# The attention mask is written into the score banks by ScalarE instead of by TensorE, and the scores are laid out by head

## The chip, the cores and the metric

One NeuronCore of a Trainium2 chip, five engines: TensorE (PE, with its weight loads as PEld), VectorE (DVE), ScalarE (ACT), GpSimd (POOL) and SyncE (SP, which issues the DMAs). The metric is the device time of one execution in microseconds, lower is better.

## What is computed

A macaron block on 2048 tokens of 128 channels, all in float32: half a stack of six layers, a retention block, the same half stack again.

```
x = x + 0.5 * stack(layernorm(x))
x = x + retention(layernorm(x))
x = x + 0.5 * stack(layernorm(x))

def stack(x):                                   # 6 layers
    for i in range(6):
        x = attention(shift_tokens(x), ...) + x
        x = ffn(shift_tokens(x), ...) + x       # layernorm, 128 -> 2*341, a * gelu(gate), 341 -> 128

def attention(x):                               # 16 heads of 64, windows of 32
    q, k, v = split(x @ Wqkv); q = l2norm(q) * qs; k = l2norm(k) * ksc
    q, k = rotary with scales
    # each window of 32 queries sees its own 32 keys and the 32 before them
    sim = 8 * q @ k.T, masked where i < j, i > j + 32 or before the first window
    out = softmax(sim) @ v;  return out @ Wo
```

Wv and Wo are folded into one matrix per head when the kernel starts, so V is projected straight into 128 outputs per head.

## The kernel before

**Tiles and slots.** Tokens are cut into 16 tiles of 128 (four windows each). A stack runs 6 x 16 = 96 tiles, one new tile per slot, in a software pipeline: in slot c the projections of tile c, the first transposes of tile c-1, the mask and scores of tile c-2, the softmax of tile c-3, the V projection of tile c-4 and the attention of tile c-5 are done. The feed-forward part works on groups of four tiles, spread over four slots: `ffn_centre` and `ffn_variance` at c % 4 = 0, `ffn_up(.., 0)` at 1, `ffn_up(.., 1)` at 2, `ffn_up(.., 2)` and the three `ffn_down` at 3. At c % 16 = 7 `ffn_bias` is added. The program is unrolled; every engine has its own list and runs it strictly in the order written; only semaphores tie the lists together. `after(...)` and `need(...)` are waits for a count. The order of the list around the change is what matters here.

**TensorE in a slot** (from L986 on): `project_qk(0)`, `ffn_up(2)`, `attend` (tile c-5), `p_transpose(4, 1)`, `project_v(0)`, `project_v(1)`, `out_transpose`, `project_qk(1)`, `qk_transpose(1, 0)` and `(1, 1)`, `project_v(2)`, `(3)`, `project_qk(2)`, `ffn_down(0)`, `project_qk(3)`, `ffn_down(1)`, `ffn_centre`, `ffn_down(2)`, `ffn_bias`, `qk_transpose(2, 3)`, `mask_scores`, `qk_transpose(1, 2)`, `ffn_up(0 or 1)`, `scores`, `p_transpose(3, 0)`, `ffn_variance`.

**ScalarE in a slot** (L479 to L540): Gelu of the third up part; the attention's output copy; `p_out(4, 1)`; `v_out(0)` (L462), `square(0)` (L442), `v_out(1)`, `square(1)`; the exponential of tile c-3 (L503); `qk_out(1, 0)`, `qk_out(1, 1)` (L456); `v_out(2)`, `square(2)`, `v_out(3)`, `square(3)`, `qk_out(2, 3)`: the last copy of transposed keys into KT; the feed-forward's square, or its Gelu (L476) between two table loads; `qk_out(1, 2)` into QT; `p_out(3, 0)`; the logarithm and exponential of the norms.

**VectorE in a slot** (L640 to L708): rotary products `rotate(0)`, `rotate(1)` (L597, L602), two square sums (L610); sums of the softmax (L651), reciprocal; `rotate(2)`, `square_sum(2)`, `square_sum(3)`, a maximum with a constant over the norms (L661); `rotate(3)`; maximum of the scores (L671) and subtraction into Z (L675), which is signalled by `s_z`; `inverse_norm`; the feed-forward's residual; `attn_residual` (L629), which waits for `out_transpose` of the next slot's TensorE list.

**GpSimd in a slot** (L358 to L378): the rotary table, `norm_mult(1, 1)` (L337), `rot_add(0)` (L330), `norm_mult(1, 2)`, `rot_add(1)`, `softmax_mult`, `last_keys` (L354, at c % 4 = 1), `rot_add(2)`, `norm_mult(1, 3)`, `rot_add(3)`, `norm_mult(0, 0)`.

**Banks.** VS is two PSUM banks of 512 columns. They hold, one after the other in a slot, the V projection's outputs (L886) and the masked scores. Head 8e + ch has its 64 scores in bank e: 32 at ch*32 for the window before and 32 at 256 + ch*32 for its own. `mask_scores` (L914) opens both banks with a product of a bf16 identity and a bf16 mask of 0 and -1e30; the 64 products of `scores` (128 records in the profile, as each float32 product takes two) are added to it. TensorE must wait for `s_te3`, the count of `qk_out(.., 3)`, before `scores`, and for `s_z` of the tile before `project_v(0)`.

## Time and profile before

| | |
|---|---|
| median of 3 runs | 3583.01 us (3582.12 to 3585.25) |
| profiled execution | 3582.17 us, span of the core 3580.4 us |
| TensorE busy | 3406.9 us, 95% of the span |
| TensorE weight loads | 1859.3 us, 52% |
| VectorE busy | 2839.3 us, 79% |
| ScalarE busy | 2383.7 us, 67% |
| GpSimd busy | 2334.5 us, 65% |
| mean granted TensorE clock | 0.974 |
| chain that ended last | 91% TensorE; of its lines the mask's L920 has 2% |

The first slots start at 101.6 us (first stack) and 1893.3 us (second); before, between and behind lie the folding of weights, the layer norms and the retention block. Busy time is a union of the profiled spans; the ends of matmuls are modelled, so spans of successive products overlap, and the price of a product is the distance between starts.

### The profile page before, as it was taken

Reading aid. Unit: us, or ns where it says so; the run is one execution under the profiler, and the core shown is the slowest. Engines: PE = TensorE matmul, PEld = TensorE weight load, DVE = VectorE, ACT = ScalarE, POOL = GpSimd, SP = SyncE. Lnnn points to the kernel's source line nnn. Section 1 sums busy time; section 2 is a strip of 40 time slices with the busy share of each in tenths; the row PEclk is TensorE's granted clock in tenths of the full one; section 3 lists DMA queues with packets and bytes.
Section 4 is the critical chain, followed back from the end, with each engine's and each line's share of the span. In section 5 each row is a group of like instructions: output and inputs, shape, how many; then the busy total and the mean of one; then the engine's idle time right before and its main releaser. Section 6 shows DMA issues by size and latency. Waiting matters only on the chain.

```text
span 3580.4 us, 123150 instructions
## 1 busy us (share of the span) xinstructions
PE 3406.9 (95%) x51660; PEld 1859.3 (52%) x51660; DVE 2839.3 (79%) x6042; ACT 2383.7 (67%) x4153; POOL 2334.5 (65%) x2187
## 2 busy tenths in 40 slices
PE   3799999999999999999797999999999999999997
PEld 2355555555555555555363555555555555555553
DVE  1788888888888888888367888888888888888883
ACT  1566776776776776776524667767777767767764
POOL 0677766767766766767046767777777767777761
PEclk7799999999999999999898999999999999999998
DMA  5000000000000000000100000000000000000000
GB/s 192 9 11 27 23 12 27 23 12 27 22 13 27 22 13 27 21 13 4 56 1 9 10 28 21 12 28 21 12 29 21 12 28 21 12 28 22 12 5 13
DMA packets 50087, 82.93 MB, mean 23 GB/s; under 512 B 7168, under 2 KB 37120, under 8 KB 47232
## 3 DMA queue, kind: packets, MB, share of 16 engines
q1 hardware_dynamic: 49536, 75.05, 6.6%
q8 instruction: 411, 6.73, 0.8%
q14 instruction: 140, 1.15, 0.1%
HBM read 67.69 MB, written 7.34 MB: 21 GB/s over the span
## 4 chain that ended last, share of the span: by engine, by line
PE 91%; DVE 3%; issue 2%; ACT 1%; DMA 1%; POOL 1%; SPq 0%; DVEq 0%; POOLq 0%; ACTq 0%
PE VS L886 20%; PE QA L826 18%; PE TB L845 10%; PE TB L910 9%; PE VS L936 7%; PE TB L869 6%; PE FB L962 4%; PE FB L963 3%; PE FB L971 3%; PE VS L920 2%; PE TB L853 1%; PE FB L952 1%; PE FB L947 1%; DMA KT<-in_w_out 1%; DVE T L602 1%
## 5 line engine op out<-in xcount | busy, mean ns | idle before, releaser
L330 POOL TENSOR_TENSOR QN<-T 128x512 f32<-128x512 f32 x768 | 980.5, 1277 | 574.4 <-DVE T L602 574.4
L337 POOL TENSOR_TENSOR QN<-QN,RR 128x512 f32<-128x512 f32 x768 | 800.9, 1043 | 295.1 <-DVE RR L623 295.1
L826 PE MATMUL QA<-WQ,Y 128*128 128x512 f32 x1536 | 796.6, 617 | 23.1 <-DVE T L602 12.0
L886 PE MATMUL VS<-MW,Y 128*32 128x512 f32 x6144 | 741.9, 601 | 5.8 <-DVE Z L675 5.8
L442 ACT ACTIVATE SQ<-QA 128x512 f32<-128x512 f32 x768 | 458.9, 597 | 269.9 <-PE QA L826 259.0
L602 DVE TENSOR_TENSOR T<-QA,TAB 128x256 f32<-128x256 f32 x1536 | 569.5, 411 | 0.0
L597 DVE TENSOR_TENSOR T<-QA,TAB 128x512 f32<-128x512 f32 x768 | 512.8, 668 | 30.6 <-ACT SQ L442 16.1
L462 ACT ACTIVATE V<-VS 128x512 f32<-128x512 f32 x768 | 461.0, 600 | 96.0 <-PE VS L886 95.4
L910 PEld LDWEIGHTS TB<-CST,QN 128*128 128x128 f32 x3072 | 374.3, 142 | 256.7 <-issue 189.1
L610 DVE TENSOR_REDUCE SSQ<-SQ 128x8 f32<-128x512 f32 x768 | 486.4, 674 | 0.0
L629 DVE TENSOR_TENSOR Y<-TB,Y 64x128 f32<-64x128 f32 x384 | 111.1, 289 | 461.8 <-PE TB L853 459.2
L346 POOL TENSOR_TENSOR Z<-Z,RC 128x512 f32<-128x512 f32 x384 | 394.4, 1048 | 121.3 <-DVE RC L655 121.3
L910 PE MATMUL TB<-CST,QN 128*128 128x128 f32 x3072 | 438.0, 275 | 15.1 <-POOL QN L337 14.4
L826 PEld LDWEIGHTS QA<-WQ,Y 128*128 128x128 f32 x1536 | 264.6, 200 | 312.9 <-DVE T L602 175.6
L845 PEld LDWEIGHTS TB<-V,PT 128*32 128x32 f32 x12288 | 326.3, 110 | 152.1 <-issue 109.3
L845 PE MATMUL TB<-V,PT 128*32 128x128 f32 x12288 | 381.8, 274 | 2.5 <-issue 1.9
L468 ACT ACTIVATE PT<-TB 128x512 f32<-128x512 f32 x384 | 228.9, 596 | 188.2 <-PE TB L869 188.1
L886 PEld LDWEIGHTS VS<-MW,Y 128*32 128x32 f32 x6144 | 161.3, 109 | 300.9 <-issue 297.9
L456 ACT ACTIVATE KT<-TB 128x512 f32<-128x512 f32 x384 | 231.6, 603 | 116.1 <-PE TB L910 116.1
L936 PEld LDWEIGHTS VS<-KT,QT 64*32 64x32 f32 x24576 | 255.2, 105 | 96.6 <-issue 79.9
L936 PE MATMUL VS<-KT,QT 64*32 64x64 f32 x24576 | 288.4, 225 | 9.1 <-issue 9.1
L671 DVE TENSOR_REDUCE MX<-VS 128x8 f32<-128x512 f32 x384 | 245.1, 677 | 29.0 <-PE VS L936 24.6
(172 smaller groups left out, 4269.7 us busy)
## 6 DMA issues: line engine op xcount, KB each, us to landing
TAB<-in_tables SPq DMA_DIRECT2D x192, 128.0 KB, 2.1
WQ<-in_w_qk SPq DMA_DIRECT2D x48, 256.0 KB, 2.9
MW<-m_dram SPq DMA_DIRECT2D x12, 1024.0 KB, 4.8
m_dram<-QN SPq DMA_DIRECT2D x6, 1024.0 KB, 4.9
W1R<-in_w SPq DMA_DIRECT2D x12, 341.0 KB, 3.1
KT<-in_w_vt SPq DMA_DIRECT2D x6, 512.0 KB, 5.8
KT<-in_w_out SPq DMA_DIRECT2D x6, 512.0 KB, 6.6
W<-in_w SPq DMA_DIRECT2D x12, 192.0 KB, 2.4
```

The costliest lines, as they stand in the source:

```text
L330: po.tensor_tensor(QN[:, n % 2, k, :], T1[:, k, :], T2[:, k, :], ALU.add).then_inc(s_add, 1)
L337: po.tensor_tensor(heads(QN[:, m % 2, k, :]), heads(QN[:, m % 2, k, :]), RR[:, m % 2, 8 * k:8 * k + 8].unsqueeze(2).to_broadcast([P, 8, DH ...
L442: nc.scalar.activation(SQ[:, k % 2, :], QA[:, k % 2, :], ACT.Square).then_inc(s_sq, 1)
L462: nc.scalar.activation(V4[:, m % 4, w, :], VS[:, w % 2, :], ACT.Copy).then_inc(s_ve, 1)
L597: nc.vector.tensor_tensor(heads(T1[:, k, :]), heads(QA[:, b, :]), tab[:, 0:DHEAD].unsqueeze(1).to_broadcast([P, 8, DHEAD]), ALU.mult)
L602: ins = nc.vector.tensor_tensor(t2[:, :, half, :], q2[:, :, 1 - half, :], tab[:, DHEAD + 32 * half:DHEAD + 32 * half + 32].unsqueeze(1).to ...
L610: nc.vector.tensor_reduce(SSQ[:, n % 2, 8 * k:8 * k + 8], heads(SQ[:, k % 2, :]), AX.X, ALU.add)\
L826: mm(QA[:, k % 2, :], Y[:, j * P:(j + 1) * P], WQ[:, k, :], start=True, stop=True).then_inc(s_qk, 1)
L845: last = mm(TB[32 * w:32 * w + 32, 1, 0:P], PT[:, m % 2, b, 32 * w:32 * w + 32], v, start=(b == 0), stop=(b == CH - 1), tile_position=(0, ...
L886: last = mm(VS[32 * q:32 * q + 32, w % 2, :], Y[:, a:a + WIN], MW[:, q, :], start=True, stop=True, tile_position=(0, 32 * q), skip_group_c ...
L910: last = nc.tensor.transpose(TB[:, (0, 1, 1, 0)[k], b * P:(b + 1) * P], QN[:, m % 2, k, b * P:(b + 1) * P], IDF)
L936: last = mm(bank[32 * w:32 * w + 32, :, ch, :], QT[r, m % 2, ch, w * WIN:(w + 1) * WIN], KT[r, ch, a:a + 2 * WIN].rearrange("p (a k) -> p ...
```

## The change

`mask_scores` and its bf16 identity go away. ScalarE writes the mask, now float32 and 64 columns per tile kind, into both banks with one copy of 128 x 1024, repeated over the 16 heads (`mask_seed`); the score products are added to what lies there. A head's 64 scores are now adjacent (ch*64 in bank e), so that one view `both` names all 16 heads over both banks, and VectorE takes one maximum of 128 x 1024 to 16 where it took two of 128 x 512 to 8. Z keeps its layout: the subtraction reads by head and writes in the old places. In ScalarE's list `v_out(3)` is moved ahead of `square(2)`, the seed stands between them, and `square(3)` is moved behind `qk_out(2, 3)`. TensorE's wait for the banks moves to ScalarE, and TensorE gets a wait for the seed.

```diff
-        MX = sb("MX", [P, 2, 2, CH])
+        MX = sb("MX", [P, 2, HEADS])
-        MASKN = sb("MASKN", [P, 2, 2, WIN], bf16)
-        IDB = sb("IDB", [P, P], bf16)
+        MASKN = sb("MASKN", [P, 2, 2 * WIN])
...
+        def both(bank):
+            return bank[:, :, :].rearrange("p e (c k) -> p (e c) k", k=2 * WIN)
...
-            sp.dma_start(MASKN[:, :, :, :], mask_n).then_inc(s_c_in, 16)
-            sp.dma_start(IDB[:, :], ident).then_inc(s_c_in, 16)
+            sp.dma_start(MASKN[:, :, :], mask_n).then_inc(s_c_in, 16)
...
+                def mask_seed():
+                    m = n - 2
+                    after(ac, s_z, 1, n - 3, 0, it, s)
+                    after(ac, s_ve, 4, n - 4, 3, it, s)
+                    nc.scalar.activation(both(VS), MASKN[:, 0 if m % TPL == 0 else 1, :].unsqueeze(1)
+                                         .to_broadcast([P, HEADS, 2 * WIN]), ACT.Copy).then_inc(s_seed, 1)
...
                 if live(c, 4, it):
                     v_out(2)
+                    v_out(3)
+                if live(c, 2, it):
+                    mask_seed()
                 if live(c, 0, it):
                     square(2)
-                if live(c, 4, it):
-                    v_out(3)
-                if live(c, 0, it):
-                    square(3)
                 if live(c, 2, it):
                     qk_out(2, 3)
+                if live(c, 0, it):
+                    square(3)
...
+                    nc.vector.tensor_reduce(MX[:, m % 2, :], both(VS), AX.X, ALU.max).then_inc(s_mx, 1)
+                    ve.wait_ge(s_mx, by_tile(1, m, it, 1))
                     for e in range(2):
-                        nc.vector.tensor_reduce(MX[:, m % 2, e, :], VS[:, e, :].rearrange(
-                            "p (a c k) -> p c a k", a=2, c=CH), AX.XY, ALU.max).then_inc(s_mx, 1)
-                    for e in range(2):
-                        ve.wait_ge(s_mx, by_tile(2, m, it, e + 1))
                         ins = nc.vector.tensor_tensor(
-                            Z[:, m % 2, e * GT:(e + 1) * GT].rearrange("p (a c k) -> p a c k", a=2, c=CH),
-                            VS[:, e, :].rearrange("p (a c k) -> p a c k", a=2, c=CH),
-                            MX[:, m % 2, e, :].unsqueeze(1).unsqueeze(3).to_broadcast([P, 2, CH, WIN]), ALU.subtract)
+                            Z[:, m % 2, e * GT:(e + 1) * GT].rearrange("p (a c k) -> p c a k", a=2, c=CH),
+                            VS[:, e, :].rearrange("p (c a k) -> p c a k", a=2, c=CH),
+                            MX[:, m % 2, CH * e:CH * e + CH].unsqueeze(2).unsqueeze(3).to_broadcast([P, CH, 2, WIN]),
+                            ALU.subtract)
...
-                def mask_scores():
-                    m = n - 2
-                    if edge:
-                        after(pe, s_z, 1, n - 3, 0, it, s)
-                    after(pe, s_ve, 4, n - 4, 3, it, s)
-                    for e in range(2):
-                        mm(VS[:, e, :].rearrange("p (a c k) -> p a c k", a=2, c=CH), IDB[:, :],
-                           MASKN[:, 0 if m % TPL == 0 else 1, :, :].unsqueeze(2).to_broadcast([P, 2, CH, WIN]),
-                           start=True, stop=False, skip_group_check=True)
...
+                    pe.wait_ge(s_seed, by_tile(1, m, it, 1))
                     pe.wait_ge(s_te3, by_tile(1, m, it, 1))
                     for ch in range(CH):
                         for e in range(2):
                             r = slice(64 * e, 64 * e + 64)
-                            bank = VS[:, e, :].rearrange("p (a c k) -> p a c k", a=2, c=CH)
                             for w in range(4):
                                 a = j * P + w * WIN
-                                last = mm(bank[32 * w:32 * w + 32, :, ch, :], QT[r, m % 2, ch, w * WIN:(w + 1) * WIN],
-                                          KT[r, ch, a:a + 2 * WIN].rearrange("p (a k) -> p a k", a=2), start=False,
+                                last = mm(VS[32 * w:32 * w + 32, e, ch * 2 * WIN:(ch + 1) * 2 * WIN],
+                                          QT[r, m % 2, ch, w * WIN:(w + 1) * WIN], KT[r, ch, a:a + 2 * WIN], start=False,
                                           stop=(ch == CH - 1), tile_position=(64 * e, 32 * w), skip_group_check=True)
...
                     qk_transpose(2, 3)
-                    mask_scores()
```

## Rows read from the trace of the kernel before

**Rows 1.** Stretches: busy time (instructions) of each engine, granted clock, DMA share.
```profile
1200.00:1600.00 400.00, 398.90 (x6358) 217.10 (x6357) 336.95 (x731) 286.14 (x502) 283.22 (x268) 1.00 0.07 20
```

**Rows 2.** What the scores' products (L936) waited for: us, times.
```profile
  issue: 89.0, 120
...
  ACT KT L456: 16.8, 100
```

**Rows 3.** Timeline, class 0: start us, us, instruction [idle before]. Transposes to scores, norm's maximum.
```profile
1099.31 0.60 PE L910 MATMUL TB<-CST,QN 128*128 128x128 f32 x4
...
1099.75 0.59 PE L920 MATMUL VS<-MASKN,IDB 128*128 128x512 bf16 x2
...
1099.95 0.60 ACT L456 ACTIVATE KT<-TB 128x512 f32<-128x512 f32 x1 [0.58 <-PE TB L910]
...
1100.18 0.60 PE L910 MATMUL TB<-CST,QN 128*128 128x128 f32 x4
...
1100.71 1.32 PEld L936 LDWEIGHTS VS<-KT,QT 64*32 64x32 f32 x128 [0.17 <-ACT KT L456]
...
1101.15 1.27 POOL L330 TENSOR_TENSOR QN<-T 128x512 f32<-128x512 f32 x1
...
1101.47 0.98 DVE L661 TENSOR_SCALAR NRM<-SSQ 128x32 f32<-128x32 f32 x1
```

**Rows 4.** Timeline, class 3: transposes to the next slot's V projection.
```profile
1084.20 0.60 PE L910 MATMUL TB<-CST,QN 128*128 128x128 f32 x4
...
1084.84 0.60 ACT L456 ACTIVATE KT<-TB 128x512 f32<-128x512 f32 x1 [1.56 <-PE TB L910]
...
1085.29 0.98 DVE L661 TENSOR_SCALAR NRM<-SSQ 128x32 f32<-128x32 f32 x1
...
1085.60 1.32 PEld L936 LDWEIGHTS VS<-KT,QT 64*32 64x32 f32 x128 [0.17 <-ACT KT L456]
...
1086.19 1.05 POOL L337 TENSOR_TENSOR QN<-QN,RR 128x512 f32<-128x512 f32 x1
...
1087.46 1.27 DVE L671 TENSOR_REDUCE MX<-VS 128x8 f32<-128x512 f32 x2
...
1088.65 1.27 DVE L675 TENSOR_TENSOR Z<-VS,MX 128x512 f32<-128x512 f32 x2
...
1090.93 0.16 PEld L886 LDWEIGHTS VS<-MW,Y 128*32 128x32 f32 x8 [0.17 <-issue]
```

**Rows 5.** Timeline, class 2: the subtraction and the V projection after it.
```profile
1070.95 1.27 DVE L675 TENSOR_TENSOR Z<-VS,MX 128x512 f32<-128x512 f32 x2
...
1074.10 0.16 PEld L886 LDWEIGHTS VS<-MW,Y 128*32 128x32 f32 x8 [0.17 <-issue]
```

**Rows 6.** Lines by form: busy us, mean ns of one | idle before. ScalarE over 1024 elements.
```profile
L503 ACT ACTIVATE Z<-Z 128x1024 f32<-128x1024 f32 x192 | 201.1, 1048 | 0.1
```

**Rows 7.** Timeline, class 1: ScalarE's chain from the V copies to the next attention.
```profile
1045.19 0.61 ACT L462 ACTIVATE V<-VS 128x512 f32<-128x512 f32 x1
...
1047.07 0.59 ACT L462 ACTIVATE V<-VS 128x512 f32<-128x512 f32 x1
...
1047.23 0.60 PE L910 MATMUL TB<-CST,QN 128*128 128x128 f32 x4
...
1048.02 0.62 ACT L456 ACTIVATE KT<-TB 128x512 f32<-128x512 f32 x1
...
1049.92 0.61 POOL L354 TENSOR_TENSOR KT<-KT,ONE 128x256 f32<-128x256 f32 x1
...
1050.25 0.32 DVE L661 TENSOR_SCALAR NRM<-SSQ 128x32 f32<-128x32 f32 x1
...
1050.52 0.69 ACT L476 ACTIVATE GE<-FB,PRB 128x512 f32<-128x512 f32 x1 [0.57 <-PE FB L963]
...
1052.52 0.60 ACT L456 ACTIVATE QT<-TB 128x512 f32<-128x512 f32 x1
...
1053.27 1.69 PEld L845 LDWEIGHTS TB<-V,PT 128*32 128x32 f32 x64 [0.76 <-issue]
```

More of the change, by code:

```diff
@@ L52, in after, with build_macaron @@
     need(engine, sem, by_tile(per, m, it, k + 1))
-def build_macaron(nc, x, w_qk, w_vt, w_out, q_rows, w1, w2, prm_ffn, w_ret, gn, tables, consts, mask_n, ident,
+def build_macaron(nc, x, w_qk, w_vt, w_out, q_rows, w1, w2, prm_ffn, w_ret, gn, tables, consts, mask_n,
                   dec_a, dec_v, m_dram, out):
-    fp32, bf16 = mybir.dt.float32, mybir.dt.bfloat16
+    fp32 = mybir.dt.float32
     ACT, ALU, AX = mybir.ActivationFunctionType, mybir.AluOpType, mybir.AxisListType
@@ L156, in build_macaron @@
         s_xn, s_h, s_y, s_prb, s_w1 = sem("s_xn"), sem("s_h"), sem("s_y"), sem("s_prb"), sem("s_w1")
-        s_sq, s_ve, s_te, s_te3, s_pe, s_ex, s_oe = (
-            sem(n) for n in ("s_sq", "s_ve", "s_te", "s_te3", "s_pe", "s_ex", "s_oe"))
+        s_sq, s_ve, s_te, s_te3, s_pe, s_ex, s_oe, s_seed = (
+            sem(n) for n in ("s_sq", "s_ve", "s_te", "s_te3", "s_pe", "s_ex", "s_oe", "s_seed"))
         s_rl, s_re, s_fsq, s_fl, s_frs, s_ge = (sem(n) for n in
@@ L508, in slot @@
                     v_out(2)
+                    v_out(3)
+                if live(c, 2, it):
+                    mask_seed()
                 if live(c, 0, it):
                     square(2)
-                if live(c, 4, it):
-                    v_out(3)
+                if live(c, 2, it):
+                    qk_out(2, 3)
                 if live(c, 0, it):
                     square(3)
-                if live(c, 2, it):
-                    qk_out(2, 3)
                 if cen_g is not None:
@@ L1040, in stack @@
                 all_slots(pe, slot, s)
-            pe.wait_ge(s_c_in, 16 * 3)
+            pe.wait_ge(s_c_in, 16 * 2)
             pe.wait_ge(s_x_in, 16)
@@ L1161, in shape_constants @@
     rq = np.arange(P) % WIN
-    mask_n = np.zeros((P, 2, 2, WIN), f32)
-    mask_n[:, :, 0, :] = np.where(rq[:, None] <= np.arange(WIN)[None, :], 0, big)[:, None, :]
-    mask_n[:, :, 1, :] = np.where(rq[:, None] >= np.arange(WIN)[None, :], 0, big)[:, None, :]
-    mask_n[0:WIN, 0, 0, :] = big
+    mask_n = np.zeros((P, 2, 2 * WIN), f32)
+    mask_n[:, :, 0:WIN] = np.where(rq[:, None] <= np.arange(WIN)[None, :], 0, big)[:, None, :]
+    mask_n[:, :, WIN:] = np.where(rq[:, None] >= np.arange(WIN)[None, :], 0, big)[:, None, :]
+    mask_n[0:WIN, 0, 0:WIN] = big
     gam = (f32(1.0) - np.exp(np.linspace(np.log(1.0 / 32.0), np.log(1.0 / 512.0), RH)).astype(f32)).astype(np.float64)
@@ L1174, in shape_constants @@
     dec_v = np.concatenate([dq[:, None, :], dk[:, None, :], hm], axis=1).astype(f32)
-    return tables, consts, mask_n, eye, dec_a, dec_v, (gch ** P).astype(f32)
+    return tables, consts, mask_n, dec_a, dec_v, (gch ** P).astype(f32)
 def kernel(**inputs):
     import numpy as np
-    import ml_dtypes
     import concourse.bacc as bacc
@@ L1185 @@
     a = {k: np.ascontiguousarray(v) for k, v in inputs.items()}
-    tables, consts, mask_n, eye, dec_a, dec_v, gch = shape_constants()
-    bf = ml_dtypes.bfloat16
+    tables, consts, mask_n, dec_a, dec_v, gch = shape_constants()
     wqkv = a["L0_ffn_Wqkv"]
@@ L1210 @@
     arrays = dict(x=a["L0_attn_x"], w_qk=w_qk, w_vt=w_vt, w_out=w_out, q_rows=q_rows, w1=a["L0_ffn_W1"], w2=w2,
-                  prm_ffn=prm_ffn, w_ret=w_ret, gn=gn, tables=tables, consts=consts, mask_n=mask_n.astype(bf),
-                  ident=eye.astype(bf), dec_a=dec_a, dec_v=dec_v)
+                  prm_ffn=prm_ffn, w_ret=w_ret, gn=gn, tables=tables, consts=consts, mask_n=mask_n,
+                  dec_a=dec_a, dec_v=dec_v)
     arrays = {k: np.ascontiguousarray(v) for k, v in arrays.items()}
```

## The prediction

> **What bounds the kernel now.** The first view is the table of stretches. Inside a stack (one pass of the six layers over 16 tiles each) TensorE is busy for 398.9 of 400 us at a granted clock of 1.00, VectorE for 337, ScalarE for 286, GpSimd for 283 [rows 1]. So the time is TensorE's own time in each slot, plus whatever it waits. A change can shorten it only by the work it takes off TensorE, and only where no wait moves in.
>
> The second view is the timeline of four successive slots, because the slots repeat with period four. I call them by c % 4: class 0 has the centring product between the projections and the transposes, class 1 has one up-projection between the transposes and the scores, class 2 has one too, and class 3 has the three down-projections before its transposes and one up-projection at its start. In the timeline the starts of `project_qk(0)` lie 15.97, 16.03, 16.03 and 18.55 us apart in the undisturbed slots of these classes (19.70 where a bias slot falls in class 3). There are 48 slots of each in the two stacks. These starts are not among the rows shown, and no term of the sum rests on them.
>
> The third view is the list of what the scores' weight load waits for: the ScalarE copy of the keys, 100 times for 16.8 us, 0.17 us each [rows 2]. That is a short wait, but it says that in half of the slots the scores start exactly when that copy lets them. In class 0 it is seen: last query/key transposes (2,3) start at 1099.31, the copy into KT starts 0.64 later and takes 0.60, the scores start 0.16 after its end at 1100.71 [rows 3]. The distance from transposes to scores is 1.40 us. Class 3 has the same 1.40 (1084.20 to the scores at 1085.60) [rows 4]. In classes 1 and 2 the up-projection's four products lie between, and nothing is waited for.
>
> **Step 1: the mask products leave TensorE.** The two products of a slot occupy it from 1099.75 to 1100.18, 0.43 us [rows 3]. Over 192 tiles that is 83 us, the most the change can bring here.
> - Classes 0 and 3: the path transposes, copy, scores is 1.40 us with or without the mask. The 0.43 us of mask work lay beside the copy. Taken away, it turns into wait: 0.17 becomes 0.60. Gain 0.
> - Class 2: transposes, up-projection and scores follow one another without a wait, and I find none to come in: the subtraction that frees the banks starts at 1070.95 and ends 1072.22, and the V projection that needs it starts at 1074.10, so it may come 0.43 earlier [rows 5]. Gain 0.43.
> - Class 1: gain 0.43 less what ScalarE's later chain costs (step 2).
>
> **Step 2: ScalarE gets the seed, and its order changes.** The new copy of 1024 elements is not in the trace. The nearest row is the exponential over 1024 elements, 1.048 us [rows 6]. I take 1.05. Below, no copy of 1024 should be shorter than the 0.60 us of a copy of 512 [rows 7]; above, two copies of 512 end to end are 1.20, and since no row shows ScalarE writing to PSUM, I let it go to 1.4. The Trainium skill ("ScalarE: Activation LUTs", What ACT_TABLE_LOAD costs) gives an instruction with immediate scale and bias as 186 ns + 0.833 ns per element, an estimate of 1.04 us; the same page, in What happens when an `exp` ACTIVATE runs, says that PSUM is the faster destination. The first agrees with the 1.048 of the exponential; no row here shows the second. By them the sum would not grow.
> What it delays, in class 1: `v_out(2)` starts at 1045.19 [rows 7]. Copies follow each other at 0.48 us (47.07 to 48.02 holds two), so `v_out(3)` runs 45.67 to 46.27. The seed waits for its end, 46.30 to 47.35. `square(2)` follows at 47.25. The key copy can start 0.64 after the transposes at 47.23, at 47.87, a little earlier than its 48.02. `square(3)` now stands behind it, 48.35 to 48.95. The table load of 1.28 us then ends at 50.25, the Gelu starts at 50.27. Without the mask the up-projection lets it start at 50.52 - 0.43 = 50.09. So it is 0.18 late, and so is everything behind it: Gelu, table load, and the copy of QT, which the attention of the next slot waits for: QT ends at 53.12 and that block starts at 53.27, 0.15 later, about the 0.16 of a handover; there is no slack. **Class 1 gains 0.43 - 0.18 = 0.25.**
> In class 2 the same chain is late by as much, but the next slot's second up-projection, four products, lies ahead of the attention, so it is covered. In class 0 the seed falls into ScalarE's 0.58 us of idleness before the key copy [rows 3] and some waiting for the projections. Cover gone, each 0.1 us would cost 4.8 us per class.
>
> **Step 3: `square(3)` stands behind the key copy.** This matters in class 3, where that copy waits 1.56 us for the transposes behind the down-projections [rows 4]. `square(3)` was over long before; now it starts at 84.84 + 0.48 = 85.32 and ends at 85.92. VectorE waits for it with the fourth square sum: 85.99 to 86.66, where the norm's maximum used to start at 85.29. That is 1.4 late. But the maximum (L661) takes 0.98 us there, 0.32 in class 1, and in the long cases it ends with a GpSimd instruction: 1101.15 + 1.27 = 1102.42 against 1101.47 + 0.98 = 1102.45 [rows 3]. So it waits for GpSimd's instruction to end. The Trainium skill ("GPSIMD Engine Reference", Specifications) says GpSimd shares its SBUF interfaces with VectorE and contends with VectorE's two-port modes; the rows agree. In the changed kernel it would arrive at 86.67, meet GpSimd's 86.19 to 87.24, and end at 87.27 instead of 86.27: the delay is 1.0, not 1.4. The maximum over the scores then starts at 88.46 instead of 87.46. In class 0 the same rule hides the delay: `square(3)` ends 0.3 later for the sum, but the norm's maximum ends with GpSimd's instruction either way. In class 1 VectorE is 0.18 late and has over 1 us to the V projection.
>
> **Step 4: VectorE's maximum and subtraction.** Two maxima take 1.19 from start to start of what follows, 1.27 to their end [rows 4]. One over both banks takes between these; but now the subtraction waits for all of it where it waited for the first half, so I take 1.24 from start to start, 0.05 more. The subtraction reads in order and writes with a stride; I take its 1.27 unchanged. No row shows a stride's price; I bound it by 0 to 1.27 (each element twice). In class 3 the end moves from 89.92 to 88.46 + 1.24 + 1.27 = 90.97. The V projection starts at 1090.93 and waits for it [rows 4]; with a handover of 0.05 to 0.16 it comes 0.15 late. **Class 3 loses 0.15.** In the bias slots the transposes come 1.2 us later and this is covered. In class 0 over 0.6 us are left.
>
> **Step 5: the rest at nothing.** The scores' products write 64 adjacent columns instead of 2 x 32; same count, same columns, and no row tells the forms apart. The seed semaphore is given over 1 us before TensorE looks at it; nothing is queued behind that wait but the scores. One start-up load fewer on SP's queue: 0 to 0.5 us once.
>
> **Sum.** Slots with a full pipeline and an up-projection: class 1 23 per stack, class 2 22, class 3 without bias 17. 46 x 0.25 = 11.5; 44 x 0.43 = 18.9; 34 x -0.15 = -5.1; together 25.3 us. The profiled execution took 3582.17 us (span 3580.4), 0.84 below the median of 3583.01. 3582.2 - 25.3 = 3556.9; from the median 3557.7. I give **3557.5 us**, 0.7% faster, about a third of the 83.
>
> **The rivals.**
> - *Port missed.* In class 1 the norm's maximum starts at 1050.25, while GpSimd's key shift runs 1049.92 to 50.53, and gets in after 0.32 us, before GpSimd's next [rows 7]. At 0.18 late it still arrives 0.1 before 50.53. If the seed takes 0.1 longer it misses, waits out 1.28 us, and the subtraction ends 0.17 too late for the V projection. 46 x 0.17 = 8 us back: 3566.
> - *Everything is taken back.* A seed of 1.4 us makes class 1 0.18 + 0.35 = 0.53 late against 0.43 gained, with the missed port as well: 18.9 - 46 x 0.27 - 5 = about 1.5 us left: 3581. For it: no row has a ScalarE write to PSUM. Against it: 1.048 for the same size.
> - *Instruction stalls move.* The scores' load waits for "issue" 120 times [rows 2]; in single slots of classes 0 and 2 the 128 records take 0.4 to 2 us longer, some 15 us in all. Five instructions fewer per slot shift where these fall. Nearly all gone: 3543; as many again: 3572.
> - *The whole 83 us.* If the key copy did not set the scores' start in classes 0 and 3: 3500. The 100 waits speak against it.
> - *Slower.* VectorE's rewritten pair costs x more than now. Class 3 pays x in full, class 0 from 0.65 on, each gated by the V projection's wait for the subtraction. At x = 1.2, nearly the bound of step 4: 34 x 1.2 + 48 x 0.55 = 67 us against 25: 3625. It decides from x = 0.65 on. For it: the subtraction gets a four-dimensional, permuted output. Against it: the four-dimensional reads of before show no penalty.
>
> **How the numbers follow.** Forecast 0.50; port missed 0.13; stalls moved by over 5 us 0.13 (two thirds of it downwards in time); all taken back 0.10; the whole gain 0.04; slower 0.10. The range takes in the forecast, the port, and the stalls both ways: 3540 to 3579; what lies out is the whole gain, the slower case and a part of the taken back. A measurement of this kernel can tell about 0.2%, 7 us, from no change. Faster by more: 0.50 + 0.13 + 0.13 + 0.04 = 0.80; within: 0.10; slower: 0.10.
>
> **What would show it.** Class 0 and 3 slots keep 15.97 and about 18.7 us, with the scores' wait for the key copy at 0.60, some 60 us in all against 16.8. Class 1 at 15.78, class 2 at 15.60. The seed row at 1.05 us. A V projection that waits for the subtraction in class 3. In class 3 the fourth square sum starts about 1.4 us later against the transposes. I am wrong if class 0 or 3 gets shorter, if the seed is over 1.2 us, or if class 2 gains less than 0.4.

## The result, and the profile after

The changed kernel takes **3611.05 us** (median of 8, 3601.07 to 3618.59), the kernel before 3582.86 us beside it (8 runs): ratio **1.0073** with a 95% interval of 1.0058 to 1.0088. It is 0.7% slower where 0.7% faster was forecast. The profiled execution took 3615.75 us.

The page of the changed kernel: the span, busy times, TensorE's program fetches (queue, packets, MB, share), the chain by engine, and two rows of the costliest groups (busy, mean ns of one, idle time before them and what ended most of it).

```profile
span 3613.8 us, 122687 instructions
...
PE 3344.2 (93%) x51276; PEld 1827.8 (51%) x51276; DVE 2869.4 (79%) x5850; ACT 2562.5 (71%) x4345; POOL 2336.1 (65%) x2187
...
q8 instruction: 408, 6.68, 0.8%
...
PE 74%; ACT 11%; issue 8%; DVE 5%; POOL 1%; DMA 1%; SPq 0%; ACTq 0%; DVEq 0%; POOLq 0%
...
L934 PE MATMUL VS<-KT,QT 64*32 64x64 f32 x24576 | 291.4, 225 | 77.6 <-issue 42.1
...
L934 PEld LDWEIGHTS VS<-KT,QT 64*32 64x32 f32 x24576 | 258.6, 105 | 171.7 <-issue 168.4
```

TensorE's busy time fell by 62.7 us (3406.9 to 3344.2), and the span grew by 33.4. So work left TensorE and more waiting came in. The list of waits says where (us in total, times, longest):

```profile
PEld VS L934 <- issue: 168.4, 216, 2.6
...
PE VS L934 <- issue: 42.1, 28, 2.5
PE VS L934 <- ACT KT L457: 35.2, 102, 0.5
...
PE TB L853 <- ACT QT L457: 6.0, 38, 0.2
```

PEld is the weight load, PE the product. The kernel before has for the same two "issue" rows:

```profile
PEld VS L936 <- issue: 79.9, 106, 2.1
...
PE VS L936 <- issue: 9.1, 14, 1.9
```

(The 89.0 us and 120 times of [rows 2], which the prediction reads as the load's, are these two together; after the change they are 210.5 us and 244 times.) The wait for the key copy (L457) comes 102 times, 0.34 us each, as forecast in kind. The row to look at is the second of the changed kernel: 28 times TensorE stops at a scores product and no other engine is named, up to 2.5 us; before it was 14 times. This is one such place, in a class 0 slot (timeline of the changed kernel: start, length, engine, line, what, idle time before it):

```profile
293.43 0.60 ACT L457 ACTIVATE KT<-TB 128x512 f32<-128x512 f32 x1 [0.81 <-PE TB L918]
...
294.17 1.44 PE L934 MATMUL VS<-KT,QT 64*32 64x64 f32 x124 [0.34 <-ACT KT L457]
...
297.54 0.30 PE L934 MATMUL VS<-KT,QT 64*32 64x64 f32 x4 [1.93 <-issue]
297.54 0.14 PEld L934 LDWEIGHTS VS<-KT,QT 64*32 64x32 f32 x3 [2.09 <-issue]
...
297.88 1.23 DVE L679 TENSOR_REDUCE MX<-VS 128x16 f32<-128x1024 f32 x1 [0.68 <-PE VS L934]
```

Elsewhere the 128 products run without a break, 1.41 us from the first of them to the instruction behind them. Here 124 are done, then comes a hole, then the last four; what they read has been there since 294.03.

I measured all slots of the trace in two ways. First, each slot's length from `project_qk(0)` to the next, by class, as a median, which leaves the holes out:

| class | before | forecast | after |
|---|---|---|---|
| 0 | 15.97 | 15.97 | 16.18 |
| 1 | 16.03 | 15.78 | 15.54 |
| 2 | 16.03 | 15.60 | 15.96 |
| 3 | 18.55 | 18.70 | 18.52 |
| sum of a cycle | 66.58 | 66.05 | 66.20 |

Second, by how much the 128 products exceed 1.41 us, summed over the 48 slots of a class: before 3.3, 0.1, 9.9 and 0.2 us for classes 0 to 3 (13.5 in all); after 18.4, 9.5, 10.0 and 16.8 (54.7). So **the undisturbed slots gained about what was forecast (0.38 us a cycle against 0.53, some 18 us against 25), and 41 us of holes inside the scores were added.** 18 off and 41 on is 23 of the span's 33 us; I don't assign the other 10. Most of them lie inside the stacks too: added up slot by slot, class 0 grew by 31 us, class 3 by 19, and classes 1 and 2 shrank by 14 and 5, 31 together. One part is that a hole also delays what follows it: behind four of the class 3 holes the attention starts 1.75 to 1.84 us into the next slot instead of 0.95.

### The profile page after: what moved, and what is told of

The parts are those of the page before. It is cut to its first block, busy times and chain, and to the rows that moved or that the text cites. A ratio compares the mean times of both kernels' runs of the same rounds, so it can differ in the third digit from the quotient of the medians.

```text
span 3613.8 us, 122687 instructions
## 1 busy us (share of the span) xinstructions
PE 3344.2 (93%) x51276; PEld 1827.8 (51%) x51276; DVE 2869.4 (79%) x5850; ACT 2562.5 (71%) x4345; POOL 2336.1 (65%) x2187
## 4 chain that ended last, share of the span: by engine, by line
PE 74%; ACT 11%; issue 8%; DVE 5%; POOL 1%; DMA 1%; SPq 0%; ACTq 0%; DVEq 0%; POOLq 0%
PE VS L894 18%; PE QA L834 15%; PE TB L853 9%; PE TB L918 6%; PE VS L934 6%; PE TB L877 5%; PE FB L969 3%; PE FB L960 3%; PE FB L961 2%; ACT KT L457 2%; ACT SQ L443 2%; PE TB L861 1%; ACT L531 1%; ACT V L470 1%; PE FB L950 1%
## 5 line engine op out<-in xcount | busy, mean ns | idle before, releaser
L894 PE MATMUL VS<-MW,Y 128*32 128x512 f32 x6144 | 739.1, 598 | 14.0 <-DVE Z L682 12.4
L619 DVE TENSOR_REDUCE SSQ<-SQ 128x8 f32<-128x512 f32 x768 | 494.1, 677 | 70.0 <-ACT SQ L443 69.5
L470 ACT ACTIVATE V<-VS 128x512 f32<-128x512 f32 x768 | 442.1, 607 | 98.1 <-PE VS L894 97.6
L918 PEld LDWEIGHTS TB<-CST,QN 128*128 128x128 f32 x3072 | 360.4, 142 | 226.9 <-issue 195.2
L347 POOL TENSOR_TENSOR Z<-Z,RC 128x512 f32<-128x512 f32 x384 | 394.4, 1048 | 123.4 <-DVE RC L664 123.4
L918 PE MATMUL TB<-CST,QN 128*128 128x128 f32 x3072 | 410.4, 276 | 17.0 <-POOL QN L338 16.3
L853 PEld LDWEIGHTS TB<-V,PT 128*32 128x32 f32 x12288 | 329.4, 110 | 166.5 <-issue 115.6
L853 PE MATMUL TB<-V,PT 128*32 128x128 f32 x12288 | 383.9, 275 | 10.0 <-ACT QT L457 6.0
L934 PE MATMUL VS<-KT,QT 64*32 64x64 f32 x24576 | 291.4, 225 | 77.6 <-issue 42.1
L457 ACT ACTIVATE KT<-TB 128x512 f32<-128x512 f32 x384 | 229.4, 597 | 176.3 <-PE TB L918 174.7
L894 PEld LDWEIGHTS VS<-MW,Y 128*32 128x32 f32 x6144 | 162.4, 109 | 310.7 <-issue 294.9
L877 PE MATMUL TB<-CST,Z 128*128 128x128 f32 x1536 | 255.4, 289 | 10.4 <-issue 9.7
```

Of the source, the lines that this page charges most:

```text
L470: nc.scalar.activation(V4[:, m % 4, w, :], VS[:, w % 2, :], ACT.Copy).then_inc(s_ve, 1)
L619: nc.vector.tensor_reduce(SSQ[:, n % 2, 8 * k:8 * k + 8], heads(SQ[:, k % 2, :]), AX.X, ALU.add)\
L853: last = mm(TB[32 * w:32 * w + 32, 1, 0:P], PT[:, m % 2, b, 32 * w:32 * w + 32], v, start=(b == 0), stop=(b == CH - 1), tile_position=(0, ...
L894: last = mm(VS[32 * q:32 * q + 32, w % 2, :], Y[:, a:a + WIN], MW[:, q, :], start=True, stop=True, tile_position=(0, 32 * q), skip_group_c ...
L918: last = nc.tensor.transpose(TB[:, (0, 1, 1, 0)[k], b * P:(b + 1) * P], QN[:, m % 2, k, b * P:(b + 1) * P], IDF)
L934: last = mm(VS[32 * w:32 * w + 32, e, ch * 2 * WIN:(ch + 1) * 2 * WIN], QT[r, m % 2, ch, w * WIN:(w + 1) * WIN], KT[r, ch, a:a + 2 * WIN], ...
```

## Experiments

**Where the holes lie.** The 408 program fetches of the page against the some 104,600 instructions of TensorE (51,276 products, as many loads, 2,029 waits) make one fetch for 256 instructions. I call what one fetch brings a page. Counting TensorE's records in order, every hole lies where such a page of 256 ends, and 26 of the 28 lie in the last 50 of the scores' 256 instructions (128 loads and 128 products). From the start of the fetch (queue 8 in the trace) to the first use of its page it takes 2.2 to 2.9 us there, mostly 2.3 to 2.7; in the slot above it starts at 295.13 and the products go on at 297.54. The question is why the fetch starts so late. The Trainium skill ("Runtime: NRT & Kernel Launch", Instruction fetch mechanics) gives the same 256 instructions and says that crossing a block's end is "mostly hidden". Here most are, and those in the scores cost up to 2.5 us each.

**The theories.** *S (a separate wait)*: the scores used to have one wait in front (the transposes' copies, s_te3; in class 2 also s_kp); now they have one more. In the trace the first load of the scores carries one wait; the other is an instruction of its own (their number rises from 1913 to 2029), which holds TensorE's sequencer, the part that issues its instructions in order, until its semaphore comes, and the next fetch starts only behind it. *P (place)*: 652 instructions fewer in all, 3.4 a slot, moved the page ends into the scores, by bad luck. *W (waits between engines)*: the holes are another engine's lateness. The first five runs tell these apart. The expectations below use the same letters.

**1. One wait.** The seed's wait at the scores is left out; the key copy stands behind the seed in ScalarE's list, so its semaphore covers both.

```diff
-                    pe.wait_ge(s_seed, by_tile(1, m, it, 1))
                     pe.wait_ge(s_te3, by_tile(1, m, it, 1))
```

> The changed kernel with one line less: TensorE no longer waits for the seed in front of the scores. It still waits for the key copy, which stands behind the seed in ScalarE's list. Theory S (a standalone wait): with two waits in front of one product, one of them becomes an instruction of its own, which holds TensorE's sequencer until the key copy is done; the next page of 256 instructions is then asked for too late, and where a page ends inside the scores TensorE stands still for 1.1 to 2.5 us. With one wait the sequencer runs ahead again: total of these stalls back from some 55 us to under 25, time 3560 to 3572 us, 0.3 to 0.6% faster than before. Theory P (alignment): the change shifts where the pages end, by chance to worse places; 192 instructions less shift them again, to no place in particular: 3580 to 3620. Theory W (waits between engines, as in the prediction's steps 2 and 3, cost more than reckoned): nothing changes, 3611.

Measured 3545.19 us, ratio 0.9889 (0.9872 to 0.9905), 15 us below what S gave. One line is worth 66 us. The holes are gone in classes 0, 1 and 3 (excess 0.1, 0.0 and 0.1 us), three are left in class 2 (3.9 us). The same slot as above, of this kernel:

```profile
293.01 1.32 PEld L933 LDWEIGHTS VS<-KT,QT 64*32 64x32 f32 x128 [0.49 <-ACT KT L457]
293.01 1.49 PE L933 MATMUL VS<-KT,QT 64*32 64x64 f32 x128 [0.25 <-ACT KT L457]
```

The scores wait for the key copy as before, then all 128 run through. ScalarE's and VectorE's work is the same (2560.4 and 2866.3 us busy, in the changed kernel 2562.5 and 2869.4), so W falls.

**2. The two lines exchanged.** Same instructions, same count, same page ends.

```diff
-                    pe.wait_ge(s_seed, by_tile(1, m, it, 1))
                     pe.wait_ge(s_te3, by_tile(1, m, it, 1))
+                    pe.wait_ge(s_seed, by_tile(1, m, it, 1))
```

> The changed kernel with the two waits in front of the scores in the other order in the program; same waits, same number of instructions on every engine, so pages end at the same places. Theory S: if the wait that now becomes the standalone instruction is the one for the seed, which is given 1.5 us or more before, the sequencer passes it early and the time falls to 3560 to 3575 us; if the same wait stays the standalone one, 3611 as before the swap. Theory P: pages end where they did, so 3611 whatever the order. Theory W: 3611.

Measured 3555.73 us, ratio 0.9918 (0.9903 to 0.9933), 4 us below the range of S: 55 us less than the changed kernel for an exchange of two lines. Its rows for the same slot and in the list of waits:

```profile
293.81 1.45 PE L934 MATMUL VS<-KT,QT 64*32 64x64 f32 x124 [0.25 <-ACT KT L457]
295.59 0.30 PE L934 MATMUL VS<-KT,QT 64*32 64x64 f32 x4 [0.33 <-issue]
```

```profile
PE VS L934 <- issue: 9.5, 14, 1.9
```

The page ends after the same 124 products, but the hole is 0.33 instead of 1.93 us, and at 14 places instead of 28 is there one at all. The place draws which slots can be hit; the order of the waits sets the price.

**3. A second wait in the kernel before**, on a semaphore that was given long ago (s_ve), nothing else.

```diff
+                    pe.wait_ge(s_ve, by_tile(4, n - 4, it, 4)) if n >= 4 else None
                     pe.wait_ge(s_te3, by_tile(1, m, it, 1))
```

> The kernel before with one more wait in front of the scores, for the V copies of an older tile, which is always fulfilled already (mask_scores has waited for the same). Nothing else is changed. Theory S: the standalone wait holds the sequencer as in the changed kernel; stalls grow from about 17 us to 50 or more, 3605 to 3640 us, 0.6 to 1.6% slower. Theory P: an instruction more per slot moves the page ends; 3575 to 3595. Theory W: same, 3583.

Measured 3619.71 us, ratio 1.0093 (1.0069 to 1.0116). The undisturbed slots keep their lengths; the excess rises to 13.7, 5.3, 9.4 and 7.1 us. Its row in the list of waits, where the kernel before has 9.1 us:

```profile
PE VS L937 <- issue: 27.6, 27, 2.4
```

So a wait that is always fulfilled makes the kernel before 36 us slower, more than the change's own 28, without any of the change. (The traced execution, 3606.82 us, is the fastest of the four, which reach up to 3627.35.) The records show how. The separate wait is recorded 0.03 to 0.04 us after the **key copy** ends, in the changed kernel (0.08 us before the scores in classes 0 and 3, 1.41 in 1 and 2) as here (0.12 and 1.73). Not the added wait holds the sequencer: the one *written last* becomes the separate instruction, and that is s_te3; the trace gives that instruction the source line of the wait written last, in the changed kernel as here and in run 2. Where a page end is hit, the fetch starts about 1.1 us behind it (1.0 to 1.6; for two of this run's 27 holes it starts before it). In run 2 the separate one is the seed's, passed 1.9 to 3.7 us before the scores (the middle value of each class).

**4. and 5. The place alone.** 32 one-column products at the start shift all page ends by 128 instructions.

```diff
             pe.wait_ge(s_x_in, 16)
+            for _ in range(32):
+                mm(TB[:, 0, 0:1], IDF, CST[:, 1, 0:1], start=True, stop=True)
```

> The changed kernel with 32 products of one column at the very start of TensorE's list, where it waits for weights anyway: 128 instructions more, half a page, so every page ends 128 instructions earlier in the program, for the whole run. Nothing else moves. It asks how much of the changed kernel's stalls is the place of the page ends. Theory S (the standalone wait sets the price of a hit, the places only how many hits there are): the hits fall on other slots, about as many, 20 to 40, 1.1 to 2.5 us each; the time stays 3595 to 3625. Theory P: the time falls to 3565 to 3585, as the bad places are left.

> The kernel before with 32 one-column products more at its start, so that TensorE's program is shifted by 128 instructions, half of what it fetches at a time; nothing else. Theory (stalls come from the late start of the fetch, the place of the page ends only draws which slots are hit): stays within 3575 to 3595. Rival (the kernel before is lucky in where its page ends fall, and the changed kernel is not): up to 3610.

Measured 3621.22 us for the changed kernel with it (ratio 1.0110, 1.0091 to 1.0129) and 3593.49 us for the kernel before with it (1.0032, 1.0020 to 1.0044). Each is 10 us slower than unshifted, and the distance between the two kernels stays 28 us. P falls as the cause.

The 10 us are not the price of the place. They are what the added products cost themselves, at the start of the program, where TensorE was not idle as the expectation of run 4 had it. The kernel before with them, and without:

```profile
8.38 13.81 PE L1045 MATMUL TB<-CST 128*128 128x1 f32 x64 [8.38 <-DMA IDB<-in_ident]
22.06 1.95 PE L1047 MATMUL QA<-CST,V 128*128 128x128 f32 x8
```

```profile
8.28 1.97 PE L1045 MATMUL QA<-CST,V 128*128 128x128 f32 x8 [8.28 <-DMA IDB<-in_ident]
```

The first slot of the first stack starts at 115.86 instead of 101.62 us in the kernel before and at 115.18 instead of 101.36 in the changed one, 14 us later. From there to the end the traced executions take 3478.3 against 3478.8 and 3510.4 against 3512.5 us. The scores' excess over 1.41 us a slot changes by 0.1 us in the kernel before and by under 4 of some 54 in the changed one, though other slots are hit. So these two runs show no price of the place that stands out of the noise.

**6. ScalarE's order alone**, in the kernel before:

```diff
                     v_out(2)
+                    v_out(3)
                 if live(c, 0, it):
                     square(2)
-                if live(c, 4, it):
-                    v_out(3)
-                if live(c, 0, it):
-                    square(3)
                 if live(c, 2, it):
                     qk_out(2, 3)
+                if live(c, 0, it):
+                    square(3)
```

> The kernel before with ScalarE's new order alone: v_out(3) ahead of square(2), square(3) behind the last key copy; no seed, mask by TensorE as before. By step 3 the norm's maximum comes 1.0 us late in class 3, the V projection 0.1 late and the transposes behind it 0.1 late: 34 slots x 0.2 = 7 us, 3587 to 3596. If the order is free, 3583.

Measured 3573.25 us, ratio 0.9973 (0.9964 to 0.9982): faster, where slower was expected. Class 0 takes 16.12 instead of 15.97, which is the 0.15 of step 3. But classes 1 and 2 take 15.97 instead of 16.03 each, since the mask products had waited 0.05 us for the last V copy, which now comes sooner; and the class 0 holes shrink from 3.3 to 1.2 us. I had priced the delay and not the copy that moved up.

**7. The layout and the single maximum alone**, with TensorE still writing the mask (by head, in two products):

```diff
+                    nc.vector.tensor_reduce(MX[:, m % 2, :], both(VS), AX.X, ALU.max).then_inc(s_mx, 1)
+                    ve.wait_ge(s_mx, by_tile(1, m, it, 1))
                     for e in range(2):
-                        nc.vector.tensor_reduce(MX[:, m % 2, e, :], VS[:, e, :].rearrange(
-                            "p (a c k) -> p c a k", a=2, c=CH), AX.XY, ALU.max).then_inc(s_mx, 1)
...
```

> The kernel before with the scores laid out by head and one maximum over both banks, the mask still by TensorE and ScalarE's order as before. By step 4 VectorE's pair costs about 0.05 us more and is covered everywhere: 3583, between 3578 and 3588. By the slower rival of the prediction the pair costs 0.65 us or more and the time is over 3600.

Measured 3582.24 us, ratio 1.0001 (0.9992 to 1.0011). This part costs nothing that can be measured.

**8. One wait, and square(3) again ahead of the key copy:**

```diff
+                if live(c, 0, it):
+                    square(3)
                 if live(c, 2, it):
                     qk_out(2, 3)
-                if live(c, 0, it):
-                    square(3)
```

> The changed kernel with one wait in front of the scores and with square(3) back in front of the last key copy in ScalarE's list. By the clean slots of the changed kernel's trace, the late square(3) costs 0.14 us at the V projection and 0.10 us at the transposes behind class 3. If step 3 of the prediction is right in kind, this kernel is 0.24 us x 34 to 44 slots = 8 to 10 us faster than the one with one wait alone: 3550 to 3562. If the order costs nothing, both are the same.

Measured 3541.73 us, ratio 0.9878 (0.9863 to 0.9893), 3.5 us under run 1 where 8 to 10 were expected. Class 0 slots fall from 16.18 to 15.86 us, 0.32 in each; but class 2 drew six holes instead of three (10.2 against 3.9 us), which takes back about half of it. So step 3's order costs 0.32 us a cycle with the seed beside it (0.15 without, run 6).

**9. The transposes earlier.** Run 8, with the transposes that feed the key copy one stage earlier in TensorE's list, so that the copy is out of the scores' way.

```diff
                     project_qk(3)
+                if live(c, 2, it):
+                    qk_transpose(2, 3)
...
-                if live(c, 2, it):
-                    qk_transpose(2, 3)
```

> The changed kernel with one wait, square(3) in front of the key copy, and the transposes (2,3) moved up to stand right behind project_qk(3), ahead of the centring product and of the last two down-projections. By step 1 the key copy is what the scores wait for in classes 0 and 3, where its wait is now 0.34 to 0.6 us; with TensorE work of 0.86 us or more between transposes and scores it is covered, and the 0.43 us of the mask that these classes gave back are gained: 96 x 0.45 = 43 us less than 3541.7, so 3490 to 3510. If something else stands right behind that wait, less than half of that: 3520 or more.

Measured 3509.58 us, ratio 0.9797 (0.9780 to 0.9813), **2% under the kernel before**. Class 0 takes 15.54 and class 3 18.12 us, 0.32 less each: the mask's work, which had turned into a wait there (step 1), is now a gain.

**10. The same move in the kernel before.**

> The kernel before with qk_transpose(2,3) moved right behind project_qk(3) and nothing else. It tells how much of the best version's gain has nothing to do with the mask. The copy of the keys is then one stage old when the scores begin, so the wait of .17 us for it in classes 0 and 3 goes, while the mask on TensorE (.5 us a slot) stays: 96 slots by .1 to .2, so 3560 to 3575. Rival: the mask waits for a VectorE copy instead and nothing is gained, 3578 to 3588.

Measured 3580.01 us, ratio 0.9993 (0.9984 to 1.0003); every class keeps its length. I expected 0.1 to 0.2 us a slot, wrongly. One such slot, class 0:

```profile
561.01 0.62 ACT L456 ACTIVATE KT<-TB 128x512 f32<-128x512 f32 x1
...
562.48 1.32 PEld L936 LDWEIGHTS VS<-KT,QT 64*32 64x32 f32 x128 [0.17 <-issue]
```

The key copy ends 0.85 us before the scores, and the load still stands idle for 0.17 us before them. The 100 waits of 0.17 us for the key copy in [rows 2] are 8 here, and "issue" has 93 more. So this 0.17 was no wait for the copy: in the kernel before TensorE's own products took as long as the copy, the two ended together, and there was nothing to win. Only without the mask products is the copy what holds the scores. The two edits pay only together.

**11. ScalarE's copies of blocks 1 and 2 ahead of its Gelus**, on top of run 9:

```diff
+                if live(c, 1, it):
+                    qk_out(1, 2)
                 if up0_g is not None:
                     gelu(up0_g, 0)
...
-                if live(c, 1, it):
-                    qk_out(1, 2)
```

> The best version so far (3509.6 us) with ScalarE's copies of query and key blocks 1 and 2 moved ahead of the two up-Gelus. In class 2 the attention product still waited .23 us for the query copy that stood behind the Gelus. Theory: that wait goes, class 2 slots fall from 15.96 to about 15.7 us, 48 of them: 11 us, so 3495 to 3502. Rival: the Gelus, now 1.5 us later, keep the down projection waiting, and the time is the same or up to 15 us longer.

Measured 3510.99 us, ratio 0.9799 (0.9784 to 0.9814): nothing. Class 2 keeps 15.96 us. The start of such a slot, in its timeline:

```profile
572.02 1.95 PE L853 MATMUL TB<-V,PT 128*32 128x128 f32 x64
...
573.48 1.29 DVE L682 TENSOR_TENSOR Z<-VS,MX 128x512 f32<-128x512 f32 x2
...
574.82 1.92 PE L894 MATMUL VS<-MW,Y 128*32 128x512 f32 x16 [0.25 <-DVE Z L682]
```

The attention (L853) no longer waits for the query copy, and now the V projection (L894) waits for the subtraction (L682), which holds its banks. One wait took another's place.

**12. Both waits again, on top of run 9**, in the changed kernel's order (seed first, transposes last):

> The best version so far (one wait at the scores, square(3) ahead of the key copy, qk_transpose(2,3) right behind project_qk(3)) with the wait on the seed put back in front of the scores, ahead of the wait on the transposes. It has 3509.6 us without that wait. Theory S1 (the stall comes only from a separate wait that TensorE's sequencer holds until the last copy is done; here the transposes are one stage old when the scores begin, so neither wait holds anything): at most 10 us more, 3508 to 3520, the scores' excess over 1.4 us stays under 4 us in every class but class 2. Theory S2 (a separate wait instruction is passed only close to the products in front of it, fulfilled or not, and what TensorE fetches of its program behind it starts only then): the stalls come back at about 1.1 us a hit in every class, 3525 to 3540.

Measured 3569.33 us, ratio 0.9960 (0.9947 to 0.9972). That is 60 us over run 9, more than either theory gave. My premise was wrong: TensorE's transposes were a stage old, but ScalarE's copy of them was not. This slot shows it:

```profile
687.23 1.03 ACT L463 ACTIVATE VS<-MASKN 128x1024 f32<-128x1024 f32 x1
688.20 1.06 ACT L443 ACTIVATE SQ<-QA 128x512 f32<-128x512 f32 x2
...
689.15 0.60 ACT L457 ACTIVATE KT<-TB 128x512 f32<-128x512 f32 x1
...
689.92 1.22 PE L934 MATMUL VS<-KT,QT 64*32 64x64 f32 x102
...
693.21 0.44 PE L934 MATMUL VS<-KT,QT 64*32 64x64 f32 x26 [2.07 <-issue]
```

The key copy stands behind the seed and two squares and ends 0.17 us before the scores, and the separate wait passes 0.04 after it. What stayed open was whether any separate wait costs this (theory F), or only the one written last, when its semaphore comes late (theory L).

**13. The same kernel with the two waits exchanged** (seed last):

> The 3569 us version (early transposes and both waits at the scores) with the two waits written in the other order: the transposes' first, the seed's last. Theory L (the wait written last becomes an instruction of its own; it is passed when its semaphore comes, and TensorE's next fetch of its program starts about 1.1 us after that): the separate wait is now the seed's, which comes 1.6 us before the scores in class 0 and over 2.5 us before them elsewhere, so a fetch starts 0.5 us before the scores in class 0 at the latest, 0.6 to 0.9 us a hit there, nothing in classes 1 and 3, class 2 as in the version without the seed's wait: 3512 to 3522. Theory F (any separate wait instruction costs the same): 3555 to 3575.

Measured 3518.04 us, ratio 0.9824 (0.9807 to 0.9841). L holds, F falls: 51 us for the order of two lines, a second time.

**14. and 15. L where the kernel before has it.** In class 2 slots the kernel before already has two waits at the scores: s_kp for the key projection, then s_te3. These are the slots with ten of its fourteen holes. (The other four lie in class 0, which has one wait there; the separate wait in front of them is that of the transposes (1,2), passed 1.4 to 1.8 us before the scores, and the fetch starts 1.0 to 1.1 us behind it.) The two lines exchanged there, in the kernel before and in run 9:

```diff
-                    if j == 0 and m % TILES:
-                        pe.wait_ge(s_kp, by_tile(1, m // 4, None) if it is None else it * 4 + m // 4)
                     pe.wait_ge(s_te3, by_tile(1, m, it, 1))
+                    if j == 0 and m % TILES:
+                        pe.wait_ge(s_kp, by_tile(1, m // 4, None) if it is None else it * 4 + m // 4)
```

> The kernel before with the two waits of its class 2 slots (the key projection's s_kp and the transposes' s_te3) written in the other order, so that s_kp, long fulfilled, comes last. Theory L: the separate wait of class 2 no longer waits for the key copy, which ends 1.77 us before these scores; the ten stalls of class 2 (9.9 us in the profile) go, those of class 0 stay: 3572 to 3577. Rival: they come from the four products in front of these scores or from where the page ends fall; nothing changes, 3580 to 3588.

> The best version so far (3509.6 us) with the same exchange in its class 2 slots. Theory L: its last 4 to 7 stalls (5.7 us in its profile, 10.6 in that of its twin a_best) go, scores' excess under 2 us in all classes together: 3500 to 3505. Rival: nothing changes, 3508 to 3512.

Measured 3574.13 us, ratio 0.9978 (0.9968 to 0.9987), and **3497.64 us, ratio 0.9768 (0.9752 to 0.9785)**, the best version: 2.3% under the kernel before. The class 2 excess falls from 9.9 to 1.9 us and from 5.7 to 0.1. Run 15 is 12 us under run 9 where 5 to 10 were expected; by the two traces 8 of them lie in class 2 slots, and I don't assign the rest. The row of waits of run 14, then of run 15:

```profile
PE VS L936 <- issue: 3.2, 5, 1.3
```

```profile
PE VS L933 <- issue: 0.2, 1, 0.2
```

28 stops of 42.1 us in the changed kernel, one of 0.2 us here.

## Why the prediction was wrong

**The step that failed is step 5**: "The seed semaphore is given over 1 us before TensorE looks at it; nothing is queued behind that wait but the scores." The first half is right (the seed ends 2.0 to 4.9 us before the scores in nearly all slots of classes 0 and 3). What I costed at nothing was not the semaphore but a second wait in front of one product. It turned the transposes' wait into an instruction that holds TensorE's sequencer, and what is queued behind that is also the fetch of the next 256 instructions. Run 1 prices it at 66 us, run 3 at 36 us in the kernel before; the forecast of 25 us off became 28 us on.

**The rival "instruction stalls move"** had the place, and the wrong mechanism and size. I gave it the shift of the places, 15 us either way, 3572 at worst; runs 4 and 5 shift them and leave the stalls' sum as it was. It had a clue that I passed over: ten of the fourteen stalls of before were in class 2, where the code writes two waits. Asking why there might have given the rule, and with the 9.9 us of ten hits spread to all four classes a rival of about 3587.

The other steps, by the changed kernel's trace:
- **Step 1, right in its result.** In classes 0 and 3 the transposes are followed by the scores after 1.38 us (1.40 before): no gain. The reading of the 0.17 us in [rows 2] as a wait for the key copy was wrong (run 10): before, TensorE's products and the copy took the same 1.40 us, and with the products away the copy's time was left. In classes 1 and 2 the mask was worth 0.49, not 0.43, since it had also waited 0.05 us for the V copy.
- **Step 2, right in kind, one slot further on.** The seed takes 1028 ns (1.05 forecast). Its wait for the query copy appears in the slot behind class 1, which my table counts as class 2: 0.23 us where 0.15 to 0.18 was forecast. The *missed port* came with it:

```profile
582.75 1.27 DVE L670 TENSOR_SCALAR NRM<-SSQ 128x32 f32<-128x32 f32 x1
...
585.23 1.96 PE L853 MATMUL TB<-V,PT 128*32 128x128 f32 x64 [0.16 <-ACT QT L457]
...
586.45 1.29 DVE L682 TENSOR_TENSOR Z<-VS,MX 128x512 f32<-128x512 f32 x2
...
587.79 0.16 PEld L894 LDWEIGHTS VS<-MW,Y 128*32 128x32 f32 x8 [0.26 <-DVE Z L682]
...
590.05 1.04 POOL L338 TENSOR_TENSOR QN<-QN,RR 128x512 f32<-128x512 f32 x1
...
590.67 1.13 PE L918 MATMUL TB<-CST,QN 128*128 128x128 f32 x8
```

  The norm's maximum takes 1.27 where it took 0.32 [rows 7], and the V projection comes another 0.09 late. The last line is a term that I missed: the query/key transposes take 1.13 instead of 1.04, about 0.10 more (GpSimd's QN ends at 591.09, while they run). 0.23 + 0.09 + 0.10 against 0.49 leaves the 0.07 of class 2 in the table.
- **Step 3, right, one slot further on.** The V projection that waits for class 3's subtraction lies in the class 0 slot behind it:

```profile
350.12 1.21 DVE L679 TENSOR_REDUCE MX<-VS 128x16 f32<-128x1024 f32 x1
...
351.37 1.29 DVE L682 TENSOR_TENSOR Z<-VS,MX 128x512 f32<-128x512 f32 x2
...
352.71 0.16 PEld L894 LDWEIGHTS VS<-MW,Y 128*32 128x32 f32 x8 [0.31 <-DVE Z L682]
```

  It starts 3.56 us into the slot where it started 3.42: 0.14 late, 0.15 forecast. The transposes again lose 0.10, not forecast; those two are class 0's 0.21 but for 0.03. (In about as many slots it starts at 3.65 and the transposes lose nothing; the sum is the same.)
- **Step 4, right.** 1.25 us from the maximum's start to the subtraction's (1.24 forecast), 1.29 for the subtraction (1.27 forecast); run 7 finds no cost. The *slower* rival on it falls.
- *The whole gain* and *everything taken back*: the undisturbed slots show neither. But run 9 shows what the first needs: the transposes moved as well.

So the undisturbed slots came near the forecast by sums and not class by class: classes 1 and 2 together gained 0.56 us (0.68 forecast), classes 3 and 0 lost 0.18 (0.15 forecast).

Of the signs that I had listed, the class 1 and 2 slots gave 15.54 and 15.96 (15.78 and 15.60 forecast): class 2 gained 0.07, and less than 0.4 was named as a sign of being wrong; what was forecast for the end of class 1 falls behind `project_qk(0)` of the next slot. The class 0 and 3 slots gave 16.18 (15.97 forecast) and 18.52, and the wait for the key copy 35.2 us in the products' row against some 60. With one wait (run 1) it is 51.0 us in the weight loads' row: in the changed kernel part of the same time goes under "issue", as the separate wait takes it.

## What to carry to other kernels

Count the waits in front of each TensorE instruction, not only when their semaphores come. Where one of TensorE's instructions needs two, write first the one that is fulfilled last, or take one away by an order that another engine's list already gives; here that was worth 51 to 66 us of 3600, two to three times what the edit could gain. A mean row that says "issue" deserves to be split by slot: what its slots have in common in the code points to the cause. A run that only shifts the program must say what the shift itself costs (runs 4 and 5). And a piece of work taken off an engine in front of a wait pays only when what it waited beside is moved too (runs 9 and 10).

## What was new about the hardware

- Of two waits written in front of the scores' first load, the last written becomes an instruction of its own (runs 2, 3, 13 and 14). It is passed 0.03 to 0.04 us after its semaphore's producer ends, and the fetch of the next 256 instructions, where one is due, starts about 1.1 us behind it (1.0 to 1.6).
- From the start of such a fetch to the first use of its instructions pass 2.2 to 2.9 us where TensorE waits for it. A run of 256 short instructions takes 1.41 us, so a fetch that starts with it comes too late: a hole, counted from product to product, of 2.0 to 2.7 us where the wait passes 0.1 us before the run, 0.9 to 1.4 at 1.4 us before it, 0.5 to 1.2 at 1.7 us.
- Shifting TensorE's program by 128 instructions has no price here that stands out of the noise; the 64 records of the products that do it take 13.7 us at the start.
- A kernel whose scores stand behind a late separate wait also scatters more from one execution to the next: 3601 to 3619 us in 8 of the changed kernel and 3560 to 3579 in 10 of run 12, but 3544 to 3546 in 4 of run 1 and 3555 to 3557 in 4 of run 2. Why is open.
- ScalarE writes 128 x 1024 elements to PSUM in 1028 ns; its exponential over as many elements in SBUF took 1048 [rows 6].
